# Attention and gated low-rank layer: the two row-sum accumulators of a head are merged by a DMA in the next head

## The reference

```python
xn = layernorm(x)
q, k, v = split(xn @ attn_qkvw + attn_qkvb)            # 32 heads of width 32
probs = softmax(q @ k.T / sqrt(32))                    # per head, 2048 x 2048
attn = (probs @ v) @ attn_ow + attn_ob
scores = (xn @ Wq_w.T) @ keys.T                        # 64 experts, the 16 highest pass a softmax
gate = spread over the 64 experts, 0 for the others
z = xn @ A_w.T                                         # 64 experts x rank 8
out = x + attn + ((z * gate) @ B_w.T) * 2.0
```

## Time and profile before

| | us |
|---|---|
| median of 3 runs | 2514.98 |
| lowest and highest | 2514.57, 2515.95 |
| the profiled execution | 2520.25 |
| its span, first to last instruction | 2518.5 |
| TensorE busy in it | 2478.8 (98%) |
| GpSimd busy in it | 1651.0 (66%) |
| VectorE busy in it | 1486.7 (59%) |
| ScalarE busy in it | 1224.5 (49%) |
| DMAs that add, issue to landing (median) | 7.7 |

### The profile page before, as it was taken

One profiled execution on the slowest core, in us unless ns is written; L12 is line 12 of the kernel. 1 busy time (PEld: TensorE's weight loads), 2 busy tenths in 40 slices (PEclk: granted clock), 3 DMA queues, 4 the chain that ended last, 5 costly groups with the idle time before them and its releaser, 6 DMA issues. The chain is left out here.

```text
span 2518.5 us, 34223 instructions
## 1 busy us (share of the span) xinstructions
PE 2478.8 (98%) x12856; PEld 1599.1 (63%) x12856; DVE 1486.7 (59%) x2524; ACT 1224.5 (49%) x2311; POOL 1651.0 (66%) x561
## 2 busy tenths in 40 slices
PE   7999999999999999999999999999999999989999
PEld 4788888888855555555555555555555555448887
DVE  7511110104588888788788888888888878521121
ACT  5211111110066667667676667666766767760000
POOL 0110111321189999999999999999999999962221
PEclk9999999999999999999999999999999999999999
DMA  4233335324368778777877777877777787564332
GB/s 167 92 125 125 118 116 162 108 80 126 97 160 165 151 159 168 156 154 166 168 148 162 165 155 155 169 150 159 168 156 154 166 167 149 120 157 138 117 104 88
DMA packets 175919, 359.50 MB, mean 143 GB/s; under 512 B 90896, under 2 KB 116448, under 8 KB 144736
## 3 DMA queue, kind: packets, MB, share of 16 engines
q0 software_dynamic: 22752, 165.69, 33.3%
q1 hardware_dynamic: 153024, 191.94, 26.8%
HBM read 127.42 MB, written 63.70 MB: 76 GB/s over the span
## 5 line engine op out<-in xcount | busy, mean ns | idle before, releaser
L1199 DVE TENSOR_REDUCE part_max<-ps_b 128x1 f32<-128x512 f32 x1984 | 1214.0, 681 | 255.1 <-PE ps_b L1072 254.9
L1021 POOL TENSOR_TENSOR psum_p<-psum_p,probs 128x2048 f32<-128x2048 f32 x253 | 1186.5, 4690 | 46.7 <-ACT probs L1185 36.9
L1185 ACT ACTIVATE probs<-ps_b 128x512 f32<-128x512 f32 x1920 | 970.9, 625 | 345.0 <-PE ps_b L1060 341.2
L1060 PE MATMUL ps_b<-q,k 128*128 128x512 f32 x1344 | 544.0, 410 | 0.0
L1072 PE MATMUL ps_b<-k,q 128*128 128x512 f32 x1344 | 534.9, 399 | 0.8
L1060 PEld LDWEIGHTS ps_b<-q,k 128*128 128x128 f32 x1344 | 250.8, 187 | 236.3 <-issue 135.8
L1090 PE MATMUL ps_b<-probs,v 128*32 128x512 f32 x2640 | 319.4, 598 | 0.5 <-ACT probs L1185 0.5
L352 POOL TENSOR_TENSOR wlo<-wraw,whi 128x1024 fp32r<-128x1024 f32 x20 | 47.9, 2397 | 404.0 <-ACT whi L527 404.0
L1060 PE MATMUL ps_b<-qk 128*128 128x512 f32 x704 | 286.4, 409 | 2.0 <-PEq L84 1.7
L1072 PEld LDWEIGHTS ps_b<-k,q 128*128 128x128 f32 x1344 | 252.6, 188 | 46.6 <-DVE part_max L1199 21.1
L1072 PE MATMUL ps_b<-qk 128*128 128x512 f32 x640 | 254.6, 398 | 0.0
(11 more groups left out here) (134 smaller groups left out, 2573.3 us busy)
## 6 DMA issues: line engine op xcount, KB each, us to landing
psum_q<-probs POOLq DMA_DIRECT2D x158, 1024.0 KB, 7.7
qk<-qk_scr SPq DMA_DIRECT2D x66, 256.0 KB, 7.4
qk_scr<-ehi SPq DMA_DIRECT2D x16, 1024.0 KB, 3.9
qk_scr<-elo SPq DMA_DIRECT2D x16, 1024.0 KB, 6.7
k<-qk_scr SPq DMA_DIRECT2D x63, 256.0 KB, 4.2
q<-qk_scr SPq DMA_DIRECT2D x63, 256.0 KB, 8.0
wraw<-wcat SPq DMA_DIRECT2D x21, 512.5 KB, 7.4
craw<-cz_scr SPq DMA_DIRECT2D x14, 768.0 KB, 4.8
```

The source lines that it names most:

```text
L1021: pool.tensor_tensor(acc[:, :], first[:, :], tile(h, t)[:, :], ALU.add).then_inc(pool_done, 1)
L1060: pe.matmul(ps[:, st_bank(n), :], kp[s][:, t * P:(t + 1) * P], qp[s][:, b * NQ:(b + 1) * NQ], start=True, stop=True).then_inc(st_ready, 1)
L1185: act.activation(tile(h, t)[:, b * NQ:(b + 1) * NQ], ps[:, st_bank(n), :], ACT.Exp, scale=SCALE).then_inc(exp_done, 1)
L1199: dve.tensor_reduce(part_max[hn % 2][:, tn, b:b + 1], ps[:, ring_bank(u), :], AX_X, ALU.max) \
```

## The change

In each of the heads 1 to 30, GpSimd issues one more adding DMA behind the addition of tile 4 (`MERGE_BEHIND`). It adds `psum_p` of the head before onto its `psum_q`. TensorE then sums `psum_q` alone, at step 10 instead of 6, and VectorE takes the reciprocals at step 13 instead of 9. The sums of the heads 30 and 31 stay as they were, in two parts and at the earlier steps. SyncE issues the load of the values ahead of the sums' spread, and the reciprocals' store and loads behind the negated maxima. The counts of the semaphore `chained` become six a head.

```diff
--- before.py
+++ after.py
@@ -62,7 +62,9 @@
 LEAD = 4
 TRANSPOSED_AT = TT - LEAD + 1
 WIDE_FROM = (HEADS - 2, TT - LEAD)
-SUMS_AT, RECIPROCAL_AT = 6, 9
+SUMS_AT, RECIPROCAL_AT = 10, 13
+LATE_SUMS_AT, LATE_RECIPROCAL_AT = 6, 9
+MERGE_BEHIND = 4
 
 OUT_KT = KT + Z_BLOCKS
 READY_KT = OUT_KT - 1
@@ -812,11 +814,21 @@
             hn, tn = (h + 1, t + LEAD) if t + LEAD < TT else (h + 2, t + LEAD - TT)
             return [(hn, tn, b) for b in range(QB)] if hn < HEADS else []
 
+        def merged(h):
+
+            return h < LAST - 1
+
+        def sums_at(h):
+            return SUMS_AT if merged(h) else LATE_SUMS_AT
+
+        def reciprocal_at(h):
+            return RECIPROCAL_AT if merged(h) else LATE_RECIPROCAL_AT
+
         ring_order = []
         for h in range(HEADS):
             for t in range(TT):
                 ring_order += [("max", *u) for u in maxima_at(h, t)]
-                if t == SUMS_AT and h >= 1:
+                if h >= 1 and t == sums_at(h - 1):
                     ring_order.append(("sum", h - 1, 0, 0))
                 if t == TRANSPOSED_AT and h < LAST:
                     ring_order.append(("flip", h + 1, 0, 0))
@@ -883,7 +895,7 @@
 
         def chain_count(h, t):
 
-            return 16 * (len(CHAIN_TILES) * (h // 2) + chain_tiles(h).index(t) + 1)
+            return 16 * ((len(CHAIN_TILES) + 1) * (h // 2) + chain_tiles(h).index(t) + 1)
 
         def based(h, t):
             return t == BASE_TILE
@@ -934,11 +946,13 @@
                 sp.wait_ge(neg_ready, h)
                 sp.dma_start(qp[s][PACK:PACK + 1, :].bitcast(F32), neg_max[h % 2][:, :]).then_inc(negmax_loaded[s], 16)
 
-            def invert_sums(h):
+            def spread_sums(h):
                 sp.wait_ge(sums_taken, h + 1)
                 for b in range(QB):
                     sp.dma_start(sums_q[b * HD:(b + 1) * HD, :], sums_b[b * HD:b * HD + 1, :]) \
                         .then_inc(sums_spread, 16)
+
+            def spread_reciprocals(h):
                 sp.wait_ge(recip_done, h + 1)
                 sp.dma_start(recip_scr.rearrange("(p c) -> p c", p=P), recip_q[:, :]).then_inc(recip_stored, 16)
                 sp.wait_ge(recip_stored, 16 * (h + 1))
@@ -981,11 +995,12 @@
                         sp.wait_ge(pv_done, TT * h + 4)
                         load_queries(h + 2)
                         clear_row(h + 2)
-                    invert_sums(h - 1)
-                    if h + 2 < HEADS:
                         load_values(h + 2)
+                    spread_sums(h - 1)
                 if h < LAST:
                     load_negmax(h + 1)
+                if h >= 1:
+                    spread_reciprocals(h - 1)
             store_ctx(LAST - 1)
             for s in range(2):
                 sp.wait_ge(ctx_stored[s], 16 * QB * (HEADS // 2 - (LAST % 2 == s)))
@@ -1036,6 +1051,12 @@
                 pool.dma_start(psum_q[h % 2][:, :], tile(h, t)[:, :], accum_op=ALU.add) \
                     .then_inc(chained[h % 2], 16)
 
+            def merge(h):
+                pool.wait_ge(pool_done, pool_adds(h + 1))
+                pool.wait_ge(chained[h % 2], chain_count(h, CHAIN_TILES[-1]))
+                pool.sem_inc(cleared, 1)
+                pool.dma_start(psum_q[h % 2][:, :], psum_p[h % 2][:, :], accum_op=ALU.add).then_inc(chained[h % 2], 16)
+
             for h in range(HEADS):
                 if h >= 2:
                     normalise(h - 2)
@@ -1046,6 +1067,8 @@
                         chain(h, t)
                     else:
                         add(h, t)
+                    if t == MERGE_BEHIND and h >= 1 and merged(h - 1):
+                        merge(h - 1)
 
         @block.tensor
         def _(pe):
@@ -1100,7 +1123,10 @@
             def sums(h):
                 u = ("sum", h, 0, 0)
                 wait_ring(pe, u)
-                pe.wait_ge(chained[h % 2], chain_count(h, CHAIN_TILES[-1]))
+                pe.wait_ge(chained[h % 2], chain_count(h, CHAIN_TILES[-1]) + (16 if merged(h) else 0))
+                if merged(h):
+                    sum_of(ring_bank(u), psum_q[h % 2], True, True).then_inc(sum_ready, 1)
+                    return
                 sum_of(ring_bank(u), psum_q[h % 2], True, False)
                 pe.wait_ge(pool_done, pool_count(h, POOL_TILES[-1]))
                 sum_of(ring_bank(u), psum_p[h % 2], False, True).then_inc(sum_ready, 1)
@@ -1221,7 +1247,7 @@
                 for t in range(TT):
                     for u in maxima_at(h, t):
                         take_max(*u)
-                    if t == RECIPROCAL_AT and h >= 1:
+                    if h >= 1 and t == reciprocal_at(h - 1):
                         reciprocal(h - 1)
                     if (h + 1, TT - 1, QB - 1) in maxima_at(h, t):
                         row_maxima(h + 1)
```

## The result

The changed kernel took 2543.89 us in the median of 4 runs (2540.6 to 2546.36), the kernel before 2514.78 beside it: a ratio of 1.0116, 95% interval 1.0104 to 1.0128. The forecast was 2505.1, the range 2489 to 2530.

What follows compares the result with a forecast made beforehand. TensorE was taken as the bound, with GpSimd taking over by 0.6 us a head: 23.1 us of added issues less 33.0 of vanishing idle time gives -9.9 us, so 2505.1 from a median of 2514.98; range 2489 to 2530.

Steps and rivals of the forecast that it cites:

- which engine takes over: Attention stage: GpSimd becomes the bound instead of TensorE, by 0.6 us a head.
- the forecast's path: GpSimd's head without idle time: 47.08 us, with the merge 47.85; time -9.9 us, chance 0.48.
- the issue: GpSimd, between the adds of tiles 4 and 5: one more DMA issue costs 0.77 us a head, 23.1 us in all.
- I take 9 to 10 ... and no wait: Landing of tile 6's DMA, in us after its issue; tile 9's DMA, due 10.1 us behind it, would not wait.
- rival 2: GpSimd at tile 9's issue: tile 6's DMA lands too late, up to 2.1 us a head, +20 us at 1 us; chance 0.20.
- landing of 8.7 us: Tile 6's DMA, if the merge and it each let one query load of about 1 us pass; no wait.
- tile 3's: Tile 3's DMA transfer, ahead of the merge on the DMA engines: ends at about 1250.5.
- idle time that was to vanish: GpSimd from 770 us to the stage's end: 30.8 us before adds and 2.2 before DMA issues, 33.0 together.
- Rival 3: VectorE at step 13: the reciprocal holds up the negated maxima, TensorE starts heads some 3 us late, +72 us; chance 0.07.

Runs made afterwards that it cites:

- merge_q0: The changed kernel with the values' load behind the sums' spread and the query loads at the head's start, ahead of the context stores: 2512.51 us, ratio 0.9993.
- v_late: The changed kernel with the load of the values put back behind the sums' spread: 2524.81 us, ratio 1.0028.
- one_sum: The kernel before, without a merge, with TensorE's sum over GpSimd's accumulator left out in heads 0 to 30: 2500.29 us, ratio 0.9933.
- one_sum_q6: one_sum with SyncE's query loads two steps later: 2496.57 us, ratio 0.9919.
- q0_only: The changed kernel with only the query loads moved to the head's start, ahead of the context stores: 2511.14 us, ratio 0.9983.
- merge_thin: The changed kernel with the merge adding only 16 of the 2048 columns, so the issue stays without its traffic: 2521.48 us, ratio 1.0017.
- alt_q0: merge_q0 with only the even heads merged: 2517.41 us, ratio 1.0007.
- the two covers: alt_q0 with the reciprocal at step 14 and GpSimd's normalising multiply behind its first addition: 2506.19 us, ratio 0.9963; again 2507.84 us, 0.9964.
- moved_q0: merge_q0 with no heads merged, both sums at step 10: 2517.85 us, ratio 1.0015.

## Why the prediction was wrong

**Right: which engine takes over.** GpSimd became the bound. TensorE, which had no waits in this stretch, now has 36.5 us of them, and GpSimd no longer waits for exponentials at its additions. merge_q0, where GpSimd waits for no landing, is the forecast's path: 47.94 us a head against 47.85. Even so the gain can't be measured: its median is 2512.51 us, ratio 0.9993 (0.9983 to 1.0004), and the profiled execution, 2506.97, is the lowest of its runs.

**Right but undersized: the issue.** 0.77 us was forecast; 29 heads of the changed kernel give 0.90 (their sum grew by 27.4 us, of which 31.0 - 29.6 = 1.4 are waits). 30 x 0.13 = 4 us more than forecast.

**Wrong: "I take 9 to 10 ... and no wait".** This is the step that failed. Tile 6's DMA landed in 10.2 us in the median of 29 heads, 8.4 to 11.3. The limit was wrong as well: I put it at 10.1 us, the time from issue to issue, but the next issue follows a landing by 0.6 us (1275.4 to 1276.0), so a wait begins at about 10.2 - 0.6 = 9.6. That is 20.2 us, 0.70 a head. The forecast had rival 2 for it, with this place and the moved load as reasons, at +20 us for 1 us a head, and gave it 0.20. What v_late took away bears it out. With the next paragraph's wait it is 1.07 us a head, so rival 2's price for 1 us a head fits only with a wait that it didn't have. The landing of 8.7 us that the prediction worked out, with one query load let past each transfer, was too short as well; no run shows how the engines take turns.

**Missed: tile 3's.** 10.8 of the 31.0 us stand one DMA earlier. The prediction let tile 3's transfer end at about 1250.5, as before, and had no wait for it. Tile 6's issue is due 10.4 us behind tile 3's in the kernel before, 11.2 with the merge between, and tile 3's DMA landed in 10.7 us in the median instead of 9.1. I treated transfers as fixed in time, while I said in the same text that TensorE would run ahead of GpSimd. SyncE's loads follow TensorE and the chain follows GpSimd, so a lead changes who is first on the DMA engines: the queries came 1.8 to 2.3 us behind tile 3's DMA before; after, they came between 0.2 us ahead and 0.5 us behind, the head shown being the latest (1253.89 against 1253.39), and there they landed in 3.9 to 8.0 us instead of 7.7 to 8.6. What they won, tile 3's DMA lost. one_sum shows it without a merge; one_sum_q6 removes the late landing, and q0_only the wait.

**The sum.** Against -33.0 us of idle time that was to vanish, from 770 us on, stand 34.3 us of new waits at DMA issues in the same heads, and 0.90 x 30 = 27 us of issues: +28 us. GpSimd's last addition came 28.5 us later, the medians give +29, and the two profiled executions +22, for the 6.3 us that the work behind it took less.

**Rival 3** did not happen in the changed kernel: TensorE waited 0.8 us for the negated maxima. In merge_thin it waited 17.5 us for them and in one_sum 16.5, but GpSimd's path set the time; in alt_q0 it stood 11.7 us behind them, and the two covers together brought 11 us.

## What to carry to other kernels

Where one engine has 1 us of slack a period and a change gives it 0.9 us of work and takes as much from the other, the engine that gains gets a lead, and every transfer that it paces moves against those of the other: ask which pair of transfers changes places or draws together. A wait on a landing has to be reckoned to the waiting issue, with the time from landing to issue in it. And a trade of 0.86 us on one engine for 0.90 on another is best made only as often as it takes to level them: of the three that were tried here (every head, every second, none) every second head was best.

## What the runs showed of the hardware

Adding DMAs issued by GpSimd and loads issued by SyncE share the engines, and how close their issues stand sets the landing: with the queries 2.1 us behind it the 1 MiB transfer of tile 3 landed in 9.5 us, with them 0.5 us behind or 0.1 us ahead of it in 10.6 and 10.4, and with them two steps later (7.9 us behind) in 7.2 in the median. It isn't the order alone: with the queries 7.6 us ahead, in moved_q0, it took 10.7. A wait for several semaphores was named after ScalarE in 27.6 of 31.0 us, though nearly all ended 0.60 us after the landing of a DMA; only the landing's own time told. And where two engines' paths were nearly equal, runs of one kernel spread: 2487 to 2522 us in ten runs of one_sum; with the queries moved, four runs on another chip gave 2492 to 2499.
